# Grouped convs and mixed-expert layers on one core: from split, rounded operands on the full array to unrounded fp32 in sixteen 32x32 tiles

## The reference, cut to what matters

```
x = x + conv9(x, W0 in 4 groups of 32 channels) + ctx0[:, :, None] + side
x = x + einsum("boi,bih->boh", sum_k att1[b,k] * e1[k], x) + att1 @ bias_k1
x = x + einsum("boi,bih->boh", sum_k att2[b,k] * e2[k], x) + att2 @ bias_k2
x = x + conv9(x, W3 in 4 groups of 32 channels) + ctx3[:, :, None] + side
```

## Time and profile before

| quantity | us |
|---|---|
| median of 3 executions | 2600.23 (2599.28 to 2600.25) |
| the profiled execution's own time | 2600.42 |
| its span, first to last instruction | 2598.5 |
| TensorE busy with matmuls in it | 2554.9 |
| VectorE busy | 2277.4 |
| ScalarE busy | 2077.8 |

### The profile page before, as it was taken

One profiled execution on the slowest core, in us unless ns is written; L12 is line 12 of the kernel. 1 busy time (PEld: TensorE's weight loads), 2 busy tenths in 40 slices (PEclk: granted clock), 3 DMA queues, 4 the chain that ended last, 5 costly groups with the idle time before them and its releaser, 6 DMA issues.

```text
span 2598.5 us, 38320 instructions
## 1 busy us (share of the span) xinstructions
PE 2554.9 (98%) x11082; PEld 2071.6 (80%) x11082; DVE 2277.4 (88%) x3384; ACT 2077.8 (80%) x1940; POOL 3.7 (0%) x17
## 2 busy tenths in 40 slices
PE   6999999999999999999999999999999999999997
PEld 4788888888888888888888888888888888888885
DVE  7988888888888888888888888888888888888884
ACT  4788878888887888888788888878888887888885
POOL 0000000000000000000000000000000000000000
PEclk8999999999999999999999999999999999999998
DMA  5788888888888888888888888888888888888875
GB/s 193 284 317 317 320 318 314 321 324 316 317 320 318 313 321 324 316 316 320 318 314 321 324 316 316 321 318 313 321 323 317 317 320 317 315 320 322 317 300 210
DMA packets 335448, 808.75 MB, mean 311 GB/s; under 512 B 37066, under 2 KB 40146, under 8 KB 302674
## 3 DMA queue, kind: packets, MB, share of 16 engines
q1 hardware_dynamic: 333200, 807.16, 83.5%
q10 hardware_dynamic: 2242, 1.53, 0.2%
HBM read 137.45 MB, written 134.22 MB: 105 GB/s over the span
## 4 chain that ended last, share of the span: by engine, by line
PE 97%; DVE 2%; issue 0%; DMA 0%; ACT 0%; ACTq 0%; SPq 0%; DVEq 0%
PE pair L766 82%; PE quad L810 14%; PE pair L800 1%; DVE mixed L595 0%; PE quad L747 0%; DMA x_in<-in_x 0%; DVE w_hi L528 0%; DVE weighted L583 0%; DVE x_lo L504 0%; DVE x_lo L630 0%; DVE x_hi L627 0%; DMA x_ph<-x_ch 0%; DVE x_ch L569 0%; DVE w_lo L534 0%; DMA x_ch<-x_ph 0%
## 5 line engine op out<-in xcount | busy, mean ns | idle before, releaser
L766 PE MATMUL pair<-x_hi,w_hi 128*128 128x512 f32 x3072 | 1227.1, 399 | 8.7 <-DVE x_lo L643 5.4
L766 PE MATMUL pair<-x_hi,w_lo 128*128 128x512 f32 x3072 | 1213.1, 395 | 0.0
L766 PE MATMUL pair<-x_lo,w_hi 128*128 128x512 f32 x3072 | 1209.0, 394 | 0.0
L766 PEld LDWEIGHTS pair<-x_hi,w_lo 128*128 128x128 f32 x3072 | 579.6, 189 | 137.3
L766 PEld LDWEIGHTS pair<-x_hi,w_hi 128*128 128x128 f32 x3072 | 579.0, 188 | 136.4 <-DVE x_lo L643 5.8
L766 PEld LDWEIGHTS pair<-x_lo,w_hi 128*128 128x128 f32 x3072 | 581.6, 189 | 131.5
L595 DVE TENSOR_REDUCE mixed<-weighted 128x128 f32<-128x1152 f32 x256 | 576.9, 2254 | 0.1
L402 ACT COPY x_out<-x_ch 128x1024 f32<-128x1024 f32 x256 | 530.3, 2073 | 2.9 <-DMA x_ch<-x_ph 2.9
L351 ACT COPY x_ch<-x_in 128x1024 f32<-128x1024 f32 x256 | 531.0, 2076 | 1.9 <-DMA x_in<-in_x 1.9
L410 ACT COPY x_ph<-pair 128x512 f32<-128x512 f32 x512 | 314.8, 615 | 272.1 <-PE pair L766 272.1
L418 ACT ACTIVATE x_ph<-pair,bias_now 128x512 f32<-128x512 f32 x512 | 358.6, 700 | 216.2 <-PE pair L766 216.2
(11 more groups left out here) (80 smaller groups left out, 607.2 us busy)
## 6 DMA issues: line engine op xcount, KB each, us to landing
x_ph<-x_ch SPq DMA_DIRECT2D x1024, 256.0 KB, 2.6
x_ch<-x_ph SPq DMA_DIRECT2D x1024, 256.0 KB, 2.6
x_in<-in_x SPq DMA_DIRECT2D x128, 1024.0 KB, 5.5
out<-x_out SPq DMA_DIRECT2D x128, 1024.0 KB, 4.2
x_out<-in_W SPq DMA_DIRECT2D x8, 144.0 KB, 5.4
expert<-in_e ACTq DMA_DIRECT2D x2, 512.0 KB, 8.0
x_ph<-in_e_t SPq DMA_DIRECT2D x1, 512.0 KB, 4.3
x_ph<-in_small ACTq DMA_DIRECT2D x1, 458.5 KB, 3.5
```

Source lines behind the costliest of these rows:

```text
L766: mm = nc.tensor.matmul(conv_bank[g % 2], w[l][:, m, g, :], x[:, g, m:m + N], start=(m == 0 and x is hi and w is w_hi), stop=(m == BLK - 1 ...
```

## The change

Both convs and the middle layers take unrounded fp32 operands, in matmuls whose stationary operand is 32x32 and whose moving operand is 32 rows x 512 columns. Rows stay channels: row strip g (partitions 32g to 32g + 31) holds group g, and column strip p of the array computes segment p of the positions (512 contiguous positions each). A tap of a conv is 16 matmuls, one in each of the 16 tiles of the array, and they write 4 PSUM banks. x1 leaves the first conv with segments as row strips and groups as banks; the middle layers read it so (for that, the middle matrix is stored to DRAM and read back 4 times into row strips, `m_rows`) and give x3 in channel rows again. All high and low parts, the cut and the join, the phase moves by DMA and the band weights are gone. The experts are added one at a time with a fused multiply-add (`mix_experts`). x1 and x4 leave PSUM half through ScalarE and half through VectorE. TensorE's step for batch b is now: 4 taps of the first conv of b (`FIRST`), a wait for x3 of b - 1, the middle matrix of b + 1, the other 5 taps, the second conv of b - 1 (9 taps), the middle of b (4 rounds of 16).

```diff
+    def rows_of(n):
+        return slice(GROUP * n, GROUP * (n + 1))
...
-        x_hi = sb("x_hi", [C, G, N + 2 * HALO], f32r)
-        x_lo = sb("x_lo", [C, G, N + 2 * HALO], f32r)
-        x1_ph = sb("x1_ph", [C, G, N])
-        x1_ch = sb("x1_ch", [C, PH, N])
-        x1_hi = sb("x1_hi", [C, PH, N], f32r)
-        x1_lo = sb("x1_lo", [C, PH, N], f32r)
-        x3_ch = sb("x3_ch", [C, PH, N])
-        x3_ph = sb("x3_ph", [C, G, N])
...
+        x_in = sb("x_in", [C, ODD, L + 2 * EDGE])
+        x1 = sb("x1", [C, G, N])
+        x3 = sb("x3", [C, L + 2 * EDGE])
+        x4 = sb("x4", [C, ODD, G, N])
+        taps = [sb(f"taps{l}", [C, TAPS, G, GROUP]) for l in range(2)]
...
-        m_hi = sb("m_hi", [C, C], f32r)
-        m_lo = sb("m_lo", [C, C], f32r)
+        m_saved = nc.dram_tensor("m_saved", [ODD, C, C], f32).ap()
+        m_rows = sb("m_rows", [C, ODD, G, C])
...
+            def save_m(b, slot):
+                sp.wait_ge(m_ready, b + 1)
+                sp.dma_start(m_saved[slot, :, :], m_t[:, :]).then_inc(m_stored, DMA)
+            def spread_m(b, slot):
+                sp.wait_ge(m_stored, DMA * (b + 1))
+                for q in range(PH):
+                    sp.dma_start(m_rows[rows_of(q), slot, :, :],
+                                 m_saved[slot, :, :].rearrange("(g c) o -> c g o", g=G)
+                                 ).then_inc(m_spread, DMA)
...
+            def step(b, slot, early=B, load_next=True, last=False):
+                if early >= 2:
+                    store(b - 2, slot)
+                if not last:
+                    save_m(b + 1, 1 - slot)
+                if load_next:
+                    load(b + 2, slot)
+                if not last:
...
+            def evacuate_x1(b, tile):
+                act.wait_ge(conv1_done, b + 1)
+                nc.scalar.copy(halves(x1, 0), halves(tile, 0)).then_inc(x1_ready[0], 1)
+            def evacuate_x4(b, slot, turn, tile):
+                wait(act, x_stored[slot], DMA * PH * turn)
+                act.wait_ge(bias4_ready, b + 1)
+                act.wait_ge(conv4_done, b + 1)
+                for g in range(G // 2):
+                    done = nc.scalar.activation(x4[:, slot, g, :], tile[:, g, :], ACT.Identity,
+                                                bias=bias4_now[:, slot, g:g + 1])
+                done.then_inc(x4_ready, 1)
+            def evacuate_x3(b, slot, tile):
+                act.wait_ge(bias3_ready, b + 1)
+                act.wait_ge(mid_done, b + 1)
+                for half in range(2):
+                    columns = x3[:, EDGE:L + EDGE].rearrange("c (p n) -> c p n", p=PH)
+                    nc.scalar.activation(halves(columns, half), halves(tile, half), ACT.Identity,
+                                         bias=bias3_now[:, slot:slot + 1]).then_inc(x3_ready, 1)
+            def step(b, slot, turn, early=B):
+                if early >= 1:
+                    evacuate_x3(b - 1, 1 - slot, banks[1 - slot])
+                evacuate_x1(b, banks[slot])
+                if early >= 1:
+                    evacuate_x4(b - 1, 1 - slot, turn - 1 + slot, banks[1 - slot])
...
-            def evacuate_x3(b):
-                act.wait_ge(bias3_ready, b + 1)
-                for half in range(2):
-                    act.wait_ge(mid_done, PH * b + PH // 2 * (half + 1))
-                    phases = slice(half * PH // 2, (half + 1) * PH // 2)
-                    nc.scalar.activation(x3_ch[:, phases, :], mid_bank[:, phases, :], ACT.Identity,
-                                         bias=bias3_now[:, :]).then_inc(x3_ready, 1)
...
+            def evacuate_x1(b, tile):
+                dve.wait_ge(conv1_done, b + 1)
+                nc.vector.tensor_copy(halves(x1, 1), halves(tile, 1)).then_inc(x1_ready[1], 1)
...
+            def mix_experts(b):
+                for k in range(K):
+                    for l in range(2):
+                        if k == 0:
+                            wait(dve, m_done, b)
+                        else:
+                            dve.wait_ge(mix_ready[l], K * b + k)
+                        nc.vector.scalar_tensor_tensor(mixed[l][:, :], expert[l][:, k, :],
+                                                       mix[l][:, b, k:k + 1],
+                                                       ident[:, :] if k == 0 else mixed[l][:, :],
+                                                       ALU.mult, ALU.add).then_inc(mix_ready[l], 1)
+            def evacuate_m(b, tile):
+                wait(dve, m_stored, DMA * b)
+                dve.wait_ge(m_done, b + 1)
+                nc.vector.tensor_copy(m_t[:, :], tile[:, PH - 1, 0:C]).then_inc(m_ready, 1)
...
+            def set_biases(b, slot):
+                wait(dve, x3_ready, 2 * (b - 1))
+                nc.vector.tensor_scalar(bias3_now[:, slot:slot + 1], bias3[:, bass.ds(b, 1)], 0.0, None,
+                                        ALU.add).then_inc(bias3_ready, 1)
+                wait(dve, x4_ready, 2 * (b - 1))
+                nc.vector.tensor_scalar(bias4_now[:, slot, :], bias4[:, :, b], 0.0, None,
+                                        ALU.add).then_inc(bias4_ready, 1)
+            def step(b, slot, turn, early=B, mix_next=True, last=False):
+                set_biases(b, slot)
+                if not last:
+                    evacuate_m(b + 1, banks[1 - slot])
+                if mix_next:
+                    mix_experts(b + 2)
+                evacuate_x1(b, banks[slot])
+                if early >= 1:
...
-            def weight_experts(b, l):
-                wait(dve, mix_ready, 2 * b + l)
-                nc.vector.tensor_tensor(weighted[:, :, :], expert[l][:, :, :],
-                                        mix[l][:, b, :].unsqueeze(2).broadcast_to([C, KI, C]),
-                                        ALU.mult).then_inc(weighted_ready, 1)
-            def sum_experts(b, l):
-                dve.wait_ge(weighted_ready, 2 * b + l + 1)
-                if l == 0:
-                    to = mixed[0][:, :].rearrange("p (c g) -> p g c", g=G)
-                    terms = weighted[:, :, :].rearrange("p k (g c) -> p g c k", g=G)
-                else:
-                    to, terms = mixed[1][:, :], weighted[:, :, :].rearrange("p k c -> p c k")
-                nc.vector.tensor_reduce(to, terms, AX.X, ALU.add).then_inc(mix_ready, 1)
...
-            def split_x1(b):
-                dve.wait_ge(x1_moved, DMA * G * (b + 1))
-                for q in range(PH + 1):
-                    if q < PH:
-                        nc.vector.tensor_copy(x1_hi[:, q, :], x1_ch[:, q, :]).then_inc(x1_high, 1)
-                    if q >= 1:
-                        dve.wait_ge(x1_high, PH * b + q)
-                        nc.vector.tensor_tensor(x1_lo[:, q - 1, :], x1_ch[:, q - 1, :],
-                                                x1_hi[:, q - 1, :].bitcast(f32), ALU.subtract
-                                                ).then_inc(x1_split, 1)
...
+            def conv_taps(l, row, tile, which):
+                for t in which:
+                    for p in range(PH):
+                        for g in range(G):
+                            mm = nc.tensor.matmul(tile[rows_of(p), g, :], taps[l][rows_of(g), t, g, :],
+                                                  row[rows_of(g), N * p + t:N * p + t + N],
+                                                  start=(t == 0), stop=(t == TAPS - 1))
+                return mm
+            def middle_matrix(b, tile):
+                pe.wait_ge(mix_ready[0], K * (b + 1))
+                pe.wait_ge(mix_ready[1], K * (b + 1))
+                nc.tensor.matmul(tile[:, PH - 1, 0:C], mixed[0][:, :], mixed[1][:, :], start=True,
+                                 stop=True).then_inc(m_done, 1)
+            def middle(b, slot, tile):
+                spread, evacuated = DMA * G * (b + 1), b + 1
+                if not isinstance(b, int):
+                    spread, evacuated = pe.to_reg(spread), pe.to_reg(evacuated)
+                pe.wait_ge(taps_ready, 1)
+                pe.wait_ge(m_spread, spread)
+                for half in range(2):
+                    pe.wait_ge(x1_ready[half], evacuated)
+                for g in range(G):
+                    for r in range(G):
+                        for q in range(PH):
+                            mm = nc.tensor.matmul(tile[rows_of(r), q, :],
+                                                  m_rows[rows_of(q), slot, g, GROUP * r:GROUP * (r + 1)],
+                                                  x1[rows_of(q), g, :], start=(g == 0), stop=(g == G - 1))
+                mm.then_inc(mid_done, 1)
+            FIRST = range(0, 4)
+            REST = range(4, TAPS)
+            def step(b, slot, turn, last=False):
+                loaded, evacuated = DMA * (turn + 1), 2 * (b - 1)
+                if not isinstance(b, int):
+                    loaded, evacuated = pe.to_reg(loaded), pe.to_reg(evacuated)
+                pe.wait_ge(taps_ready, 1)
```

(32 more changed lines are left out.)

614 lines of the change are left out of this document (179 added, 435 removed).

## The result

The changed kernel takes 3649.7 us (median of 4, 3641.0 to 3653.7), the kernel before 2599.9 on the same chip: 1.403 times as long, 95% interval 1.401 to 1.406. The prediction was 2820, 8% more than before, where 40% more was measured. The profiled execution took 3647.1 us with a span of 3645.3.

What follows compares the result with a forecast made beforehand. TensorE was taken as the only bound, limited by issuing pairs: 21.12 + 0.50 = 21.62 us a batch, times 128 is 2767, plus 50 for the ends and 1.9 around the span, so 2820 us, 8% slower; range 2500 to 3900.

Steps and rivals of the forecast that it cites:

- the ends: Opening and close of the kernel, outside the steady batches: 50 us in the sum, bounds 45 to 70.
- What leaves pays nothing by itself: Phase moves, splits, cut and join, hidden under TensorE: removal worth 0 in the loop, some microseconds at the ends.
- The stream in one tile: In a tile, one pass of 512 columns takes 0.4467 us; 44 rounds a batch would take 19.65 us.
- The issue of the pairs: On TensorE, each weight load with its matmul costs 30 ns to issue; 704 pairs make 21.12 us a batch.
- Middle matrix and change of tiles: Rest of a batch on TensorE: 0.22 us of full-array records plus 0.28 for switching from and to tiles, together 0.50.
- the loop is refetched: Rival: TensorE's long loop body is fetched anew, 2.6 us in each of 63 turns, 164 us in all; chance 6%.
- the gap every second batch: Sign of refetching expected in the changed profile: a gap on TensorE every second batch.
- thousands: Sign expected in the changed profile if the loop is refetched: instruction packets in the thousands.
- Tiles hardly overlap: Rival: matmuls in different tiles wait for each other, 10,100 or 20,200 us; chance 15% for all above 3900 us.
- Array-bound at its best, faster: Rival: issue keeps up and a record costs 0.4317 us, 19.36 us a batch, 2530 us in all; chance 25%.
- VectorE's fused multiply-add: Each of 16 in VectorE's queue ahead of its x1 copy takes 0.279 us, 4.5 us in all, hidden under taps.

Runs made afterwards that it cites:

- the kernel of 6: Changed kernel with one batch, not two, in TensorE's loop body, the previous batch's middle layers after the first four taps: 3097.1 us, 1.191 times before.
- 4: Changed kernel with TensorE's batches written out without a branch, and nearly all loads of x and stores of the result left out: 3027.7 us.
- 1: Changed kernel with all TensorE batches written out, so no branch there; other engines keep their loops: 3205.0 us, 1.232 times before.
- 9: Changed kernel with each tile matmul on bfloat16 constants, one pass in place of two, 4 experts mixed, output not the reference's: 1235.0 us.
- 7: The kernel of 6 with a tap's sixteen matmuls in another order, each next one in another row and column group: 3106.8 us.
- 8: The kernel of 6 with every tile matmul of the loop on 256 of 512 columns, 4 experts mixed: 1985.9 us.
- the kernel of 5: Changed kernel with the middle layers as matmuls of 32x128 in place of 32x32, still a loop of two batches: 3285.2 us; without the branch 3131.1.
- experiment 3: Changed kernel with each tile matmul of the loop on 256 of 512 columns, same instructions in number and order: 3437.1 us.

## Why the prediction was wrong, point by point

The direction was right and the size wrong: 220 us more were forecast, 1,050 came. The step that failed is the instruction supply. The sum has no term for it: it stood among the rivals only, at 2.6 us a turn and 6%, and it cost 550 us, 7.1 us a turn at the branch and the rest in late packets. The second is the price of a pair, 33.1 ns and not 30, worth 268 us. With 10 us more for the ends that is nearly all of the error of 830. That the measured time still lies between 2500 and 3900 us is luck: the upper part of that range was there for pairs of up to 42 ns, and a pair took 33.1.

- **What leaves pays nothing by itself:** right. No other engine stands in the chain. The ends take 3095.1 - 128 x 23.71 = 60 us in the kernel of 6, against 50.
- **The stream in one tile (0.4467 us):** the first two rounds of 32 pairs after a break take 0.88 us in the records' starts, 2 x 0.44. As a bound it was right, but it isn't kept up.
- **The issue of the pairs (30 ns):** this step failed as a mechanism. The row it rested on, a load and its matmul 30 ns apart, is one pair on an idle array and no rate; single-pass pairs come every 13.6 ns. It failed as a size by little: with the code in place a batch takes 23.71 us and the middle matrix 0.42 of it, 23.29 / 704 = 33.1 ns a pair. That is worth 128 x (23.71 - 21.62) = 268 us of the error.
- **Middle matrix and change of tiles (0.50):** 0.42 in the chain.
- **The rival "the loop is refetched":** this is what happened, and it is the larger part of the error, 550 us. Its mechanism and the gap every second batch were as written. The "thousands" of packets were not, though the prediction's own numbers give some 700 (11 a turn); there are 827. Its price was wrong threefold. A turn costs 7.1 us and not 2.6: a pause of 4.2 us, about as long as one packet's turn in the queue (the packets start 4.0 us apart, median) and longer than the 2.6 us of a move in the kernel before, and then 2.7 us of low clock, which the prediction had not at all. And outside the branch too the packets are only just in time, which costs 111 to 180 us beside data traffic without any branch. The chance of 6% was too low: the body had grown from some 170 to 2,824 instructions, the one quantity of the change that went up by more than ten. The Trainium skill (Runtime: NRT & Kernel Launch, Instruction fetch mechanics), cited in the prediction, warned of the stall, and the trace agrees. A loop body can't use its 2048 instructions for PE (8 blocks of 256) in full, as 1,800 were fetched anew; whether the figure itself holds is open, since a body of 7.0 packets with the two more that are fetched beyond it would not fit in 8, and one of 5.5 would. It calls the crossing of a block "mostly hidden": that agrees with 4, and not with 1, where TensorE waited for 84 us at the taps.
- **Tiles hardly overlap:** wrong. The starts of sixteen matmuls lie 7 ns apart after a break and 17 ns in the steady stream. The Trainium skill (TensorE: Matmul & The Clock Gate, Part 3) has 4 ns for one wave; the fp32 rows have 7 at best, and the single-pass rounds of 9 come near it, 3.3 ns behind a break.
- **Array-bound at its best, faster:** not reached. With two passes in each tile and the code in place the best is 3062.7 us.
- **VectorE's fused multiply-add (0.279):** 0.344, without effect, since VectorE is busy for 26%.

The sum, mended: 128 x 23.71 + 60 = 3095; + 550 for fetching = 3645. By the other cut of the 550: 439 for the branches and 111 by which the kernel without a branch stands above the one-batch kernel (3206.1 - 3095.1). The one-batch kernel stands in turn 69 us above the quiet one (3095.1 - 3025.9), 23.71 against 23.23 us a batch; whether data traffic or its other order makes that was not tested.

**What stays open.** Why a round of two passes in each of sixteen tiles takes 1.04 us and not 0.88. It isn't the order of tiles (7), nor the columns (8), nor the supply of instructions (6), nor the rate of single-pass pairs (9), with the reserve that 9 changed the type of the operands too. In the records' starts most of the 32 pairs of a round follow each other at 16 to 18 ns, and in three places the matmuls stand still for about 0.2 us, and the places move from round to round. That fits a queue in which one load waits for a tile that is still busy with its first pass and holds up the fifteen others, but no run showed the cause. Why the pause at the branch is 1.2 us in the kernel of 5 and 4.2 to 5.3 in the others is open too. Nor was the length between 1,412 and 1,800 at which a body ceases to stay looked for.

## What to carry to other kernels

Count the instructions of a loop body as a resource of its own: when a change multiplies them (an fp32 matmul is four in these traces, a 4x4 tiling is sixteen matmuls for one), look at the instruction queue's packets first, and keep the body at some 1,400 or less, with one batch in a turn or wider tiles. Ask then at what rate the engine eats instructions: at 16 ns each (4.15 us / 256, experiment 3) a fetched stream is on the edge here, and data traffic pushed it over. A pause is paid twice where the clock falls behind it.

## What the runs showed of the hardware

| TensorE's loop body | instructions | packets of 16 KB | packets fetched in the run |
|---|---|---|---|
| one batch, wide middle | 1,220 | 4.8 | 20 |
| two batches, 3 taps | 1,288 | 5.0 | 16 |
| one batch | 1,412 | 5.5 | 22 |
| two batches, single pass | 1,412 | 5.5 | 17 |
| two batches, 5 taps | 1,800 | 7.0 | 570 |
| two batches, 7 taps | 2,312 | 9.0 | 687 |
| two batches, wide middle | 2,440 | 9.5 | 700 |
| two batches (the changed kernel) | 2,824 | 11.0 | 827 |

- A body that was too long wasn't kept in part: all of it and 1.4 to 2 packets more were fetched in each turn. In the changed kernel fetching went one packet at a time, each in transfer for about 1.0 us. No kernel here fetched faster on average than 4.15 us a packet (3), though single packets followed each other more closely (3.8 us in the median of 3).
- A pause of 4 us of TensorE brought its granted clock to 0.66 over the next 8 us, where the same kernel had 1.00 a little later. In the fp32 kernels without such pauses it was 0.993 to 0.999 over the run.
- Sixteen 32x32 tiles take a pair of load and pass every 13.6 ns with one pass a matmul (bfloat16), and one every 33.1 ns with two (fp32), 512 columns each.
